# A cross-attention block: probabilities turned by DMA block exchange and 32x32 transposes instead of by the matrix engine

## The reference

```python
def _L0_xattn_ref(query, key):
    a = jnp.einsum('bqd,bkd->bqk', query, key)
    e = jax.nn.softmax(a, axis=-1)
    return jnp.einsum('bqk,bkd->bqd', e, key)

x = x + _L0_xattn_ref(_layernorm(x, axis=-1), ctx_4096)      # (1,256,2048), (1,25088,2048)
x = x + _L0_attn_ref(_layernorm(x, axis=-1), Wq, bq, Wk, bk, Wv, bv)
x = x + _L0_ffn_ref(_layernorm(x, axis=-1), W_base, b_base, W_gate, A, B)
```

## Time and profile before

| | |
|---|---|
| median of 3 runs | 2488.42 us (2483.71 to 2494.42) |
| the profiled execution | 2496.61 us, its span 2494.9 us |
| mean granted TensorE clock | 0.995 |
| busy: PE / DVE / ACT / POOL | 98% / 79% / 44% / 57% |
| HBM read and written | 488.7 and 28.8 MB |

### The profile page before, as it was taken

One profiled execution on the slowest core, in us unless ns is written; L12 is line 12 of the kernel. 1 busy time (PEld: TensorE's weight loads), 2 busy tenths in 40 slices (PEclk: granted clock), 3 DMA queues, 4 the chain that ended last, 5 costly groups with the idle time before them and its releaser, 6 DMA issues.

```text
span 2494.9 us, 36102 instructions
## 1 busy us (share of the span) xinstructions
PE 2443.1 (98%) x11446; PEld 2011.2 (81%) x11446; DVE 1963.5 (79%) x2702; ACT 1098.1 (44%) x1577; POOL 1416.6 (57%) x1056
## 2 busy tenths in 40 slices
PE   6999999999999999999999999999999999999799
PEld 5888888888888888888888888888888888868577
DVE  8888888888878888888888888888878888674356
ACT  4444444444444444444444444444444444443443
POOL 2766666666666555566565565555656656552341
PEclk9999999999999999999999999999999999999899
DMA  9988888788888988888988888888898888878533
GB/s 237 255 213 229 219 207 231 207 232 217 205 231 217 224 216 217 211 220 204 230 215 201 220 218 218 216 212 220 206 228 210 208 218 218 214 158 156 130 121 100
DMA packets 421367, 518.22 MB, mean 208 GB/s; under 512 B 54470, under 2 KB 296134, under 8 KB 418504
## 3 DMA queue, kind: packets, MB, share of 16 engines
q1 hardware_dynamic: 411336, 475.66, 78.1%
q0 software_dynamic: 9984, 41.95, 5.1%
HBM read 488.71 MB, written 28.84 MB: 207 GB/s over the span
## 4 chain that ended last, share of the span: by engine, by line
PE 93%; SPq 3%; DMA 2%; DVE 1%; ACT 0%; issue 0%; ACTq 0%; DVEq 0%
PE ps L1457 30%; PE ps L1459 30%; PE ps L1458 30%; PE ps L1466 2%; SPq L439 1%; DMA q_t<-qk_dram 1%; SPq L567 1%; DMA quart<-in_ctx_dram 1%; PE ps L1686 0%; PE ps L1632 0%; PE ps L1759 0%; PE ps L1485 0%; DVE acc L1203 0%; DMA qk_dram<-q_nat 0%; SPq L432 0%
## 5 line engine op out<-in xcount | busy, mean ns | idle before, releaser
L618 POOL TENSOR_TENSOR nat_lo<-raw,nat_hi 128x512 fp32r<-128x512 f32 x784 | 1171.0, 1523 | 862.3 <-ACT nat_hi L778 830.2
L1082 DVE TENSOR_TENSOR ch_lo<-tr,ch_hi 128x512 fp32r<-128x512 f32 x784 | 762.2, 972 | 296.9 <-ACT ch_hi L767 293.2
L767 ACT CAST ch_hi<-tr 128x512 fp32r<-128x512 f32 x784 | 481.1, 621 | 796.9 <-PE ps L1459 776.9
L1457 PE MATMUL ps<-ch_hi,xt_hi 128*128 128x512 f32 x1696 | 673.1, 397 | 9.9 <-DVE ch_lo L1082 6.4
L1459 PE MATMUL ps<-ch_hi,xt_lo 128*128 128x512 f32 x1696 | 662.9, 391 | 0.0
L1458 PE MATMUL ps<-ch_lo,xt_hi 128*128 128x512 f32 x1696 | 662.2, 390 | 0.0
L1457 PE MATMUL ps<-nat_hi,pt_hi 128*128 128x512 f32 x1568 | 610.3, 389 | 1.6 <-DVE pt_lo L1023 1.6
L1459 PE MATMUL ps<-nat_hi,pt_lo 128*128 128x512 f32 x1568 | 610.3, 389 | 0.0
L1458 PE MATMUL ps<-nat_lo,pt_hi 128*128 128x512 f32 x1568 | 610.0, 389 | 0.0
L1078 DVE STREAM_TRANSPOSE tr<-quart 128x512 f32<-128x512 f32 x784 | 547.6, 699 | 2.1 <-DMA quart<-in_ctx_dram 2.1
L778 ACT CAST nat_hi<-raw 128x2048 fp32r<-128x2048 f32 x196 | 374.4, 1910 | 206.7 <-PE ps L1459 184.0
(11 more groups left out here) (200 smaller groups left out, 1397.8 us busy)
## 6 DMA issues: line engine op xcount, KB each, us to landing
quart<-in_ctx_dram SPq DMA_DIRECT2D x392, 512.0 KB, 8.4
raw<-in_ctx_dram SPq DMA_DIRECT2D x196, 1024.0 KB, 8.2
wq_in<-in_L_attn_Wq_dram POOLq DMA_DIRECT2D x16, 1024.0 KB, 6.4
win<-in_L_ffn_W_base_dram SPq DMA_DIRECT2D x64, 256.0 KB, 6.8
tr<-wt_dram POOLq DMA_DIRECT2D x64, 256.0 KB, 3.2
wt_dram<-stage SPq DMA_DIRECT2D x32, 256.0 KB, 5.5
wt_dram<-stage_b SPq DMA_DIRECT2D x32, 256.0 KB, 10.3
wq_dram<-wq_out POOLq DMA_DIRECT2D x16, 256.0 KB, 2.3
```

The costliest lines, as they stand in the source:

```text
L618: last = pool.tensor_tensor(nat_lo[:, j, t], raw[:, j % 2, t], nat_hi[:, j, t].bitcast(F32), ALU.subtract)
L767: act.copy(ch_hi[:, c % RING_CH, :], tr[:, c % RING_TR, :]).then_inc(chunk_hi, 1)
L1082: dve.tensor_tensor(ch_lo[:, c % RING_CH, :], tr[:, c % RING_TR, :], ch_hi[:, c % RING_CH, :].bitcast(F32), ALU.subtract).then_inc(chunk_s ...
L1457: pe.matmul(out_, a_hi, b_hi, start=start, stop=False)
```

## The change

For every block but the first two and the last, the probabilities are no longer transposed on TensorE. ScalarE writes the exponential with its columns in another order; behind each exponential it issues four DMA transfers (`move_probs`), each of which moves a block of 128 columns of all 128 rows to 32 partitions of the new tile quads. VectorE transposes quads in 32x32 blocks back into probs (`turn_probs`), writing every fourth word. pt_hi and pt_lo are then made from SBUF. Two late row pieces, some pieces, additions and row pieces move by one chunk, VectorE's order inside an iteration changes (addition, probabilities, then the next chunk's transpose), and TensorE waits for each tile's pt_lo at that tile's first piece. quads shares its room with b_nat, so all eight loads of b_nat go behind the last block's pt_lo.

```diff
@@ -160,6 +160,7 @@
         b_nat = put(at_b, "b_nat", [P, DC, ER])
+        quads = put(at_b, "quads", [P, TT, QR, P])
@@ -380,6 +382,7 @@
+                self.by_dma = not (self.first or self.second or self.over)
@@ -407,7 +410,7 @@
-        PIECE_AFTER = {5: 0, 7: 1, 9: 2, 11: 3, 13: 4, 15: 5}
+        PIECE_AFTER = {6: 0, 8: 1, 9: 2, 11: 3, 13: 4, 15: 5}
@@ -519,8 +522,6 @@
             next_block(REST[0], LAST_M)
-            for e in range(EXPERTS // 2):
-                load_expert(e)
@@ -533,7 +534,8 @@
             sp.dma_start(x_nat[:], x_dram).then_inc(x_again, 16)
-            for e in range(EXPERTS // 2, EXPERTS):
+            sp.wait_ge(lo_drained, G_PT + TT * (NB - 1))
+            for e in range(EXPERTS):
                 load_expert(e)
@@ -781,14 +783,28 @@
-                act.activation(probs[:, q, :], ps[:, SCORE_BANK + TT * new + q, :], ACT.Exp,
+                to, of = probs[:, q, :], ps[:, SCORE_BANK + TT * new + q, :]
+                if turn.by_dma:
+                    to = to.rearrange("p (b t j) -> p t b j", b=QR, t=KT)
+                    of = of.rearrange("p (t b j) -> p t b j", b=QR, t=KT)
+                act.activation(to, of, ACT.Exp,
                                bias=neg_max[:, new, q:q + 1],
             def probs_group(turn, q):
-                hi_group(turn.times(TT, G_PT + q - TT), q, pt_hi[:, q], bank4(q))
+                if turn.by_dma:
+                    act.wait_ge(out_ready, turn.times(8, 6 + q + 1 - 16))
+                    hi_group(turn.times(TT, G_PT + q - TT), q, pt_hi[:, q], probs[:, q].rearrange("p (t m) -> p t m", t=KT))
+                else:
+                    hi_group(turn.times(TT, G_PT + q - TT), q, pt_hi[:, q], bank4(q))
+
+            def move_probs(turn, q):
+
+                act.wait_ge(probs_ready, turn.times(TT, q + 1 - TT))
+                for b in range(QR):
+                    act.dma_start(quads[b * SQ:(b + 1) * SQ, q], probs[:, q, b * P:(b + 1) * P]).then_inc(probs_moved[q], 16)
@@ -798,17 +814,19 @@
-            ROWS = {11: 0, 15: 1}
+            ROWS = {12: 0, 15: 1}
-                late = {} if turn.first else {8: 2, 11: 3} if turn.second else {LEAD: 2, 7: 3}
+                late = {} if turn.first else {8: 2, 11: 3} if turn.second else {4: 2, 7: 3}
                         for q in range(TT):
                             softmax(turn, q)
+                            if turn.by_dma:
+                                move_probs(turn, q)
@@ -1130,12 +1148,19 @@
+            def turn_probs(turn, q):
+
+                dve.wait_ge(probs_moved[q], turn.times(16 * QR, -16 * QR))
+                dve.transpose(probs[:, q].rearrange("p (t i a) -> p t a i", t=KT, a=QR),
+                              quads[:, q].rearrange("p a (t j) -> p t a j", t=KT)).then_inc(group_done, 1)
+
             def probs_group(turn, q):
-                lo_group(turn.times(TT, G_PT + q - TT), pt_lo[:, q], bank4(q), pt_hi[:, q])
-            ADD_AFTER = {9: 0, 11: 1, 13: 2, 15: 3, 17: 4}
+                src = probs[:, q].rearrange("p (t m) -> p t m", t=KT) if turn.by_dma else bank4(q)
+                lo_group(turn.times(TT, G_PT + q - TT), pt_lo[:, q], src, pt_hi[:, q])
+            ADD_AFTER = {10: 0, 12: 1, 13: 2, 15: 3, 17: 4}
@@ -1160,14 +1185,17 @@
                     lo_chunk(turn.times(DC, c), c)
+                    if c in ADD_LATE_AFTER and lagging:
+                        add_late_piece(turn, ADD_LATE_AFTER[c])
+                    if c == (7 if turn.second else 5) and not turn.first:
+                        if turn.by_dma:
+                            for q in range(TT):
+                                turn_probs(turn, q)
+                        for q in range(TT):
+                            probs_group(turn, q)
                     n = c + AHEAD
                     if n < DC or not turn.last:
                         transpose_chunk(turn.times(DC, n), n, turn.times(16 * QR, 16 * QR * (n // DC)))
-                    if c == (7 if turn.second else 5) and not turn.first:
-                        for q in range(TT):
-                            probs_group(turn, q)
-                    if c in ADD_LATE_AFTER and lagging:
-                        add_late_piece(turn, ADD_LATE_AFTER[c])
@@ -1513,7 +1541,9 @@
-                if v == 0:
+                if turn.by_dma and v < TT:
+                    pe.wait_ge(lo_drained, turn.times(TT, G_PT - 1 + v))
+                elif v == 0:
@@ -1540,7 +1570,7 @@
-                    if c == (3 if turn.second else 1) and not turn.first:
+                    if c == 3 and turn.second:
                         for q in range(TT):
                             probs_group(turn, q)
```

More of the change, by code:

```diff
@@ L307, in perceiver_block @@
         probs_ready = sem("probs_ready")
+        probs_moved = [sem(f"probs_moved{q}") for q in range(TT)]
         alpha_ready = sem("alpha_ready")
```

## The result

| | before | after |
|---|---|---|
| median of 4 runs | 2487.92 us (2483.71 to 2494.42) | 2708.31 us (2705.96 to 2716.41) |
| profiled span | 2494.9 us | 2704.9 us |
| mean granted clock | 0.995 | 0.956 |

The ratio is 1.0877 [1.0851, 1.0904]: 220 us slower. The forecast was 36 us slower, with 2565 as the upper end of the range. The direction was right, the size was not, and the range missed it.

What follows compares the result with a forecast made beforehand. TensorE's instruction count was taken as the bound: 42 us saved, 47 x 1.5 = 71 us of stalls and 5 at the end added, +35 on the profiled 2496.6, so 2524 us at the median; range 2446 to 2565.

Steps and rivals of the forecast that it cites:

- ScalarE's issues: Eight DMA issues a block at 0.38 us each, 3.0 us in all, in front of chunk 4's hi copy.
- Bound and gain: TensorE's instruction count sets the block time; removing its transposes gains 0.89 us a block, 42 us over 47 blocks.
- Rival 3: ScalarE's issues cost 0.48 us each, making the chain 0.8 us later a block: 2562 us; chance 0.10.
- Stall one: TensorE waits 0.9 us a block before chunk 6, because VectorE's subtraction for that chunk ends late.
- The transposes: VectorE's two new 128x512 transposes a block take 0.70 us each, with nothing added for writing every fourth word.
- the far bound: Strided writes cost each of VectorE's two new transposes a second 0.7 us, 1.4 us a block.
- One engine at a time: VectorE's subtractions of SBUF operands, now including pt_lo, wait for GpSimd's running subtraction, then need 0.6 us.
- Landing: The exchange's transfers land 2.3 us after issue on ScalarE's own queue, three us before VectorE's transposes want them.
- rival 4: The exchange lands 10.3 us after the last issue, delaying VectorE 4.6 us a block: about 2740 us; chance 0.04.
- Stall two: TensorE waits 0.6 us a block before chunk 8, because VectorE's subtraction for that chunk ends late.
- The granted clock: No term in the sum; time lost at a lower granted clock was named only as a sign against the forecast.
- The end: All eight b_nat loads behind the last block's pt_lo delay TensorE's last pieces about 5 us (bounds 0 and 8).

Runs made afterwards that it cites:

- The fill run: Changed kernel plus 13 matmuls into a PSUM bank nobody reads, ahead of chunk 6's scores: 2653.92 us, 1.0667 of the kernel before.
- the first run there: Changed kernel with its eight transfers a block issued by SyncE, ahead of its other work for the block: 2496.85 us, 1.0029 of the kernel before.
- the last run: Changed kernel, SyncE issuing the transfers, ahead of the loads of W, late row piece behind the exponentials: 2461.71 us, 0.9871 of the kernel before.

## Why the prediction missed

Two steps failed: the price of ScalarE's issues, which was too low, and the clock after an idle time, for which the sum had no term.

- **Bound and gain.** Right. Where the other engines keep up, the period is 43.52, and 0.89 us a block is gone.
- **ScalarE's issues: 3.0 us predicted, 5.2 measured.** This is the term of the sum that was mis-sized first. One issue takes 0.62 us (median), with the gap 0.65, against 0.38 in the prediction and 0.48 as its bound; a store's issue and a quarter load's issue were the nearest rows, and both were too cheap. ScalarE's late row piece ended at T+8.7, not 6.7, and everything behind it is late by the same 2.0: GpSimd's burst began at T+8.8 (predicted 6.7), pt_lo ended at 15.4 (13.3), chunk 6's subtraction at 16.6 (14.5). Rival 3 was this mechanism, but its price stopped at 0.8 us.
- **Stall one: 0.9 us predicted, 3.26 measured** (2.93 in the block shown). The timetable was right in its order and in what waits for what; put 2.1 us later it gives 3.0.
- **The transposes: 0.70 predicted, 1.09 measured.** The choice of GpSimd's strided addition as the nearest row failed: writing every fourth word costs VectorE's transpose 0.39 us, a bit over half of the way to the far bound of 0.7. The rule of the Trainium skill that the prediction set aside (*SBUF — State Buffer*, Specifications: each access that crosses to a new 16-byte line pays) agrees with this. It cost little in time, 17 us, since the burst's end decided for pt_lo.
- **One engine at a time.** Right: VectorE's subtraction of two SBUF operands took 1.36, and pt_lo 1177 ns on average (up to 1765) with the burst beside it, against 684 where the burst was elsewhere.
- **Landing: harmless, but not for the reason given.** The median was 3.0 us (2.3 taken) and VectorE waited for it once. The prediction took ScalarE's queue to be clear of SyncE's loads. In 15 blocks, those where four loads of W and a row load are in flight, it was not: tile 0's transfers took 7.3 to 8.5 us there on ScalarE's queue and 6.8 to 8.1 on SyncE's, and in the blocks between 2.7 to 4.1 on either. What the prediction drew from the Trainium skill (*DMA: Bandwidth & Descriptors*, Arbitration), that by the round-robin between queues the transfer would not wait for SyncE's backlog, these runs do not bear out. One such block of the changed kernel (the one above), then one of the run with SyncE's issues:

```profile
DMA to landing us min/median/max: 5.5/7.0/8.5
```

```profile
DMA to landing us min/median/max: 6.0/7.0/8.0
```

  That is the mechanism of rival 4. It stayed hidden because ScalarE's and VectorE's steps in front of the transposes took longer still; with the issues on SyncE it came out.
- **Stall two: 0.6 us predicted, absent.** TensorE's slow stretch let VectorE catch up. Where chunk 6 came sooner and no slow stretch followed (row piece behind chunk 6's copy) it appeared, 1.03 us; five of the six blocks of that run that had the slow stretch before chunk 8 have no second gap.
- **The granted clock: missing altogether.** The sum took a microsecond of idle time as a microsecond. It cost 3.26 and then 2.03 more, 95 us in the 47 blocks. The prediction named a lower clock only as what would prove it wrong. The fill run shows that it follows from the gap. The error of the first term made the gap so long that the clock fell in every one of the 47 blocks; behind the gaps of 1.0 us in the run with the row piece behind chunk 6's copy it did not. So the two errors multiplied.
- **The end: 5 us predicted, none seen.** From the start of the last block's first exponential to the end it is 317.6 us, against 318.7 before.

In one line: 2.2 us of issue time that rows of another form did not show, on a path that passes three engines in series, became 2.4 us more idle time, and that in turn 2 us of lower clock.

## What to carry to other kernels

A DMA's issue is work of the engine that makes it, and its length depends on the form of the transfer; put it on an engine with nothing behind it, and look at what loads are in flight when it is issued, on whatever queue. Draw the path across all engines before adding to any of them: two additions that each cost little (1.3% and 0.3%) can together cost 8.8%. And price a gap of TensorE with what may follow it: here the clock added six tenths of the gap again.

## What the runs showed of the hardware

- The clock fell after each of the changed kernel's long gaps (2.76 us and more), but the length of a gap alone does not tell. After one of 2.40 us (the run that issued the loads of W earlier) TensorE went on at the full clock, and once even after one of 2.93 us (the run with the row piece ahead of the exponentials, at 160.39); after one of 1.87 us (the run with half of the issues) it went on at the full clock for four matmuls, and then at the lower one. What decides in between is open. The first and the third in PE's timeline:

```profile
1659.93 0.50 PE L1486 MATMUL ps<-ch_hi,xt_hi 128*128 128x512 f32 x1 [2.40 <-DVE ch_lo L1101]
1660.27 0.39 PE L1487 MATMUL ps<-ch_lo,xt_hi 128*128 128x512 f32 x1
1660.49 0.40 PE L1488 MATMUL ps<-ch_hi,xt_lo 128*128 128x512 f32 x1
```

```profile
1716.29 0.50 PE L1495 MATMUL ps<-ch_hi,xt_hi 128*128 128x512 f32 x1 [1.87 <-DVE ch_lo L1110]
...
1718.04 0.63 PE L1495 MATMUL ps<-nat_hi,pt_hi 128*128 128x512 f32 x1
1718.47 0.63 PE L1496 MATMUL ps<-nat_lo,pt_hi 128*128 128x512 f32 x1
```

- The issue of a 64 KB transfer from 128 rows to 32 partitions takes 0.60 to 0.62 us on SyncE and on ScalarE; a store of 128 rows takes 0.333.
- A 128x512 transpose on VectorE takes 0.70 us dense and 1.09 writing every fourth word. Reading with that interleaving undone (stride of 32 words) takes ScalarE's copy from 0.62 to 1.14 us.
- The exchange's median landing was the same on either engine's queue: 3.0 us on ScalarE's (the changed kernel) and 3.1 on SyncE's (the first run there), 2.2 on ScalarE's (row piece ahead of the exponentials) and 2.2 on SyncE's (the last run).
